# AdaLN and an eight-expert MoE on one core: the copy of x into the output as one transfer, started earlier, and one VectorE step moved ahead of another

## The chip, the cores and the metric

The kernel runs on one core of a Trainium2 chip. Its time is the device time of one execution in microseconds (us). The kernel before was timed three times: 1524.31, 1526.02 and 1527.0 us, with a median of 1526.02 us. The engines are called by the names of the profile: PE (TensorE, the matrix engine; PEld is its weight load), DVE (VectorE), ACT (ScalarE), POOL (GpSimd) and SP (SyncE, which here only issues transfers). All transfers, whoever issues them, run on the core's 16 DMA engines.

## The reference, cut to what matters

```
styles = w @ (affine_w * gain).T + affine_b            # 8 x 512
y      = einsum('blc,oc->blo', x * styles, weight) * rsqrt(sum((weight*styles)**2)) 
y      = clip(y + bias, -256, 256)                     # 4096 tokens of 512
scores = softmax(y @ Wr)                               # 8 experts
G, idx = top_k(scores.T, 1024)                         # each expert takes 1024 tokens
h      = gelu(einsum('ekd,edh->ekh', y[idx], W1) + b1) # 512 -> 2048
X_e    = einsum('ekh,ehd->ekd', h, W2) + b2            # 2048 -> 512
out    = x + zeros.at[idx].add(G * X_e)                # x is the kernel's input
```

The last line is what the change touches: the output holds a copy of the input x, 4096 rows of 512 float32 (8.39 MB), to which each expert's rows are added.

## The kernel before, in words

Every matmul is done on float32 values split into a high and a low part ("hi", "lo"), three matmuls for one product. The parts are made by ACT (hi, a copy) and DVE (lo, a subtraction), and PE waits for both by semaphores. The five engines each run a list of instructions that is written out by hand, so the order in the code is the order on the engine, and a waiting instruction holds up all that stand behind it on its engine.

Stages, with their times in the profiled execution: the style matmuls and the router (to about 130 us), the choice of expert 0's tokens (to about 166 us), expert 0 in 32 blocks of work (to about 345 us), then seven more experts, each with a hidden part (8 steps of seven products, a Strassen-like scheme in which DVE adds products in PSUM) and an output part (16 chunks).

Expert 0. Block i has a matmul group `A(i)` (12 matmuls, line 1548) and a group `B(i-2)` (12 matmuls, line 1593); between them PE takes a small step of the threshold search for the other experts (`count`, lines 1485 and 1487), which needs DVE's counts (line 1031). ACT makes, in this order, the hi part of W1 for block i+2 (`w1_hi`, line 666), the hi part of W2 (`w2_hi`, line 674) and the two gelus (lines 806, 807). DVE makes, in this order, `w1_lo` (line 1129), `w2_lo` (line 1134), the lo part of the hidden values (line 1289) and then the counts of the search. The weights come by 256 KB loads that SP issues (`load_w1`, line 369; `load_w2`, line 374), three buffers each; among them SP issues transposes of gathered rows (`transposes`, line 437).

POOL gathers expert 0's rows in eight indirect transfers (line 529), and then copies x into the output in four pieces of 1024 rows (line 560). The first piece waits for the second round of SP's transposes (`s_xt`), and piece q for `A(7 + 2q)` of PE (`s_A`). All later writes to the output (the scatters, line 544) wait for all four pieces (`s_o0`).

Experts 1 to 7. In step g the DVE does `u2`, `c12` of the step before, `u3` (line 1217: product 7 plus product 1 into U3) and `c22_c21` (line 1222: adds U3 to two banks). PE's product `P3(g)` adds into one of these banks and waits for `c22_c21(g)` (semaphore `s_cc`). At the end of the hidden part (k = 7) PE runs P1, P6, P3 of the step before, P7, P5, P4, P2, then the first tile of the first output chunk (`chunk(16 * n, (0,))`, line 1664), then `P3(8 * n + 7)`, then the rest of the chunk. DVE makes the lo parts for that first chunk in `chunk_lo` (lines 1234 and 1238), once ACT has made the hi parts (`chunk_hi`, lines 767 and 771).

Of the kernel before, what the change touches and what calls it, by code (L numbers as in the profile page):

```python
# [5 lines left out]
def adaln_moe_kernel(nc, xT, x, condT, WT, biasT, affWT, affbT, WrT, W1, b1T, W2, b2, out):  # L6
# [26 lines left out]
    with ctx:  # L33
# [3 lines left out]
        def sem(name):  # L37
            return ctx.enter_context(nc.semaphore(name))
# [172 lines left out]
        def asf(ap):  # L211
            return ap.bitcast(f32)
# [9 lines left out]
        def w2slot(j):  # L222
            return RG[:, j % 2, 0:1024].rearrange("p (l n) -> p l n", l=2)

        def hslot(j):
            return RG[:, j % 2, 1024:3072].rearrange("p (l n) -> p l n", l=2)
# [51 lines left out]
        s_xt = [sem(f"s_xt{i}") for i in range(4)]  # L278
# [7 lines left out]
        s_o0 = sem("s_o0")  # L286
# [26 lines left out]
        s_A = sem("s_A")  # L313
# [32 lines left out]
        s_gat = [sem(f"s_gat{i}") for i in range(4)]  # L346
# [127 lines left out]
        def _(eng):  # L474
# [79 lines left out]
                gather(c, 0, c)  # L554

            for i in range(4):
                eng.wait_ge(s_xt[i], 32)
            for q in range(4):
                eng.wait_ge(s_A, 8 + 2 * q)
                eng.dma_start(out[1024 * q:1024 * q + 1024, :], x[1024 * q:1024 * q + 1024, :]).then_inc(s_o0, 16)  # L560
            eng.wait_ge(s_o0, 64)
            for t in range(4):
                scatter(t, 0, t, OB[:, t, :])
            gather_pairs(0)
# [292 lines left out]
        def _(eng):  # L857
# [247 lines left out]
            def build_oh(e, q):  # L1105
                if e:
                    eng.wait_ge(s_im, 4 * e)
                if e == 2 and q == 0:
                    eng.wait_ge(s_sc, 128)
                eng.tensor_tensor((OH0 if e < 2 else OHx)[:, q, :, :],  # L1110
                                  (slo[:, 8 * q:8 * q + 8, e:e + 1] if e else
                                   slo0[:, 8 * q:8 * q + 8, None]).broadcast_to([128, 8, 128]),
                                  io128[:, None, :].broadcast_to([128, 8, 128]), ALU.is_equal).then_inc(s_oh, 1)

            def finish_idx(e):
                eng.wait_ge(s_im, 4 * e + 4)
                v = list_bank(e)[:, 0:40].rearrange("p (v h) -> p h v", v=5)
                with nc.allow_low_precision(reason="token numbers below 4096 are exact"):
                    eng.tensor_reduce(idx[:, e, :], v[:, :, 0:2], AX.X, ALU.add).then_inc(s_idx, 1)
                eng.tensor_reduce(G[:, e, :], v[:, :, 2:5], AX.X, ALU.add).then_inc(s_imc, 1)  # L1120
# [16 lines left out]
            def x_lower(r):  # L1137
                eng.wait_ge(s_xt[r % 4], 16 * (r // 4 + 1))
                if r < 10:
                    if r >= 2:  # L1140
                        eng.wait_ge(s_xh, r - 1)
                        eng.wait_ge(s_xl, r - 1)
                else:
                    eng.wait_ge(s_xhr, (r - 8) // 2)
                    eng.wait_ge(s_xlr, (r - 8) // 2)
                if r >= 16 and (r - 8) % 8 == 0:
                    eng.wait_ge(s_hlo, 2 * (r - 8) - 16 + 6)
                eng.tensor_copy(halves(r)[:, :, 0], XU[:, r % 4, 4:8, :].rearrange("p c n -> p (c n)")).then_inc(s_il, 1)
# [29 lines left out]
            def sums(g):  # L1178

                u = g + 8 * (g // 8)  # L1180
                r = RAW[:, u % 3, :, :]
                eng.wait_ge(s_raw[u % 3], 32 * (u // 3 + 1))
                if g:
                    eng.wait_ge(s_wls, g)
                else:
                    eng.wait_ge(s_A, NBLK)
                chain[0] += 1
                first = chain[0]
                eng.tensor_tensor(ST[:, 0, :], r[:, 0, :], r[:, 1, :], ALU.add).then_inc(s_v, 1)
                eng.tensor_tensor(ST[:, 2, :], r[:, 0, :], r[:, 2, :], ALU.subtract)  # L1190
                eng.wait_ge(s_v, first)
                link(eng.tensor_tensor(ST[:, 1, :], ST[:, 0, :], r[:, 2, :], ALU.subtract))
                eng.tensor_tensor(ST[:, 3, :], r[:, 3, :], ST[:, 1, :], ALU.subtract).then_inc(s_sS, 1)

            def lo_raw(g):
                u = g + 8 * (g // 8)
                eng.wait_ge(s_whr, g + 1)
                eng.tensor_tensor(wslot(g)[:, 1, 0:3, :], RAW[:, u % 3, 1:4, :], asf(wslot(g)[:, 0, 0:3, :]),  # L1198
                                  ALU.subtract).then_inc(s_wlr, 1)

            def lo_S(g):
                eng.wait_ge(s_whs, g + 1)
                eng.wait_ge(s_sS, g + 1)
                eng.tensor_tensor(wslot(g)[:, 1, 3:7, :], ST[:, :, :], asf(wslot(g)[:, 0, 3:7, :]),  # L1204
                                  ALU.subtract).then_inc(s_wls, 1)

            def banks(g):
                return (Pt, BBt)[g % 2]

            def u2(g):  # L1210
                eng.wait_ge(s_cp1, g + 1)
                eng.wait_ge(s_P[6], g + 1)
                eng.tensor_tensor(U2(g), banks(g)[:, PB, :], P1C, ALU.add).then_inc(s_u2, 1)

            def u3(g):
                eng.wait_ge(s_P[7], g + 1)
                eng.tensor_tensor(U3, banks(g)[:, PB, :], P1C, ALU.add).then_inc(s_u3, 1)

            def c22_c21(g):
                eng.wait_ge(s_P[4], g + 1)  # L1220
                eng.wait_ge(s_u3, g + 1)
                eng.tensor_tensor(banks(g)[:, PB:PD + 1, :], banks(g)[:, PC:PD + 1:2, :],
                                  U3[:, None, :].broadcast_to([128, 2, 512]), ALU.add).then_inc(s_cc, 1)

            def c12(g):
                eng.wait_ge(s_P[3], g + 1)
                eng.wait_ge(s_u2, g + 1)
                eng.tensor_tensor(banks(g)[:, PC, :], banks(g)[:, PC, :], U2(g), ALU.add).then_inc(s_c12, 1)

            def chunk_lo(jj):  # L1230
                n, j = jj // 16, jj % 16
                u = 16 * n + 8 + j // 2
                eng.wait_ge(s_v2h, jj + 1)
                eng.tensor_tensor(w2slot(j)[:, 1, :], RAW[:, u % 3, :, :].rearrange("p b n -> p (b n)")  # L1234
                                  [:, 512 * (j % 2):512 * (j % 2) + 512], asf(w2slot(j)[:, 0, :]),
                                  ALU.subtract).then_inc(s_v2l, 1)
                eng.wait_ge(s_hh, jj + 1)
                eng.tensor_tensor(hslot(j)[:, 1, :], H[:, j, :], asf(hslot(j)[:, 0, :]),  # L1238
                                  ALU.subtract).then_inc(s_hlo, 1)
# [84 lines left out]
            for n in range(NX):  # L1324
                for k in range(8):
                    g = 8 * n + k
                    if 0 < k < 7:
                        lo_raw(g + 1)
                    u2(g)
                    if k:  # L1330
                        c12(g - 1)
                    else:
                        sums(g + 1)
                        lo_raw(g + 1)
                    if k == 5 and n + 2 < E:
                        finish_idx(n + 2)
                    u3(g)
                    if k == 7:
                        chunk_lo(16 * n)
                    if k < 7:  # L1340
                        lo_S(g + 1)
                    if n + 2 < E and 1 <= k <= 4:
                        build_oh(n + 2, k - 1)
                    c22_c21(g)
                    if k < 6:
                        sums(g + 2)
                c12(8 * n + 7)
                for j in range(1, 16):
                    chunk_lo(16 * n + j)
                    if n + 3 < E and j == 3:  # L1350
                        build_rhs(n + 3)
                    if n + 1 < NX and j in (6, 8, 10, 12):
                        x_lower(16 + 8 * n + j - 6)
                        x_lower(17 + 8 * n + j - 6)
                        xp_sums(4 * n + 4 + (j - 6) // 2)
                    if n + 1 < NX and j in (7, 9, 11, 13):
                        xp_lo(4 * n + 4 + (j - 7) // 2)
                    if j == 14 and n + 1 < NX:
                        sums(8 * n + 8)
                if n + 1 < NX:  # L1360
                    lo_raw(8 * n + 8)
                for t in range(4):
                    evac(n, t)
                if n + 1 < NX:
                    lo_S(8 * n + 8)
                for t in range(4, 8):
                    evac(n, t)
# [389 lines left out]
```

## Time and profile before

| | before |
|---|---|
| median of 3 runs | 1526.02 us |
| the profiled execution's own time | 1526.02 us |
| its span | 1523.8 us |
| outside the span | 2.2 us |
| PE busy | 1467.0 us, 96% |
| DVE busy | 1005.5 us, 66% |
| ACT busy | 729.8 us, 48% |
| POOL busy | 190.4 us, 12% |
| mean granted PE clock | 0.982 |
| bytes moved | 164.40 MB, mean 108 GB/s |

How to read it: the span runs from the first to the last instruction of the profiled execution. "Busy" is the time in which an engine executes; "idle before" is what it waited for. The clock is the share of full speed that was granted to PE. A transfer's "landing" is the time from its issue to its completion semaphore. A busy share near 1 in a stretch says that the stretch is bound by that engine.

### The profile page before, as it was taken

The numbers are of one execution on the slowest core, as the hardware profiler recorded it, in microseconds if no ns is written. First come the engines' busy times: TensorE is split into PE (matmuls) and PEld (weight loads), VectorE is DVE, ScalarE is ACT, GpSimd is POOL, SyncE is SP. The second block draws the span as 40 slices with busy tenths as digits, with TensorE's granted clock in tenths as the row PEclk, the third lists the DMA queues.
The fourth block names the chain that finished last, engine by engine and source line by source line (L and its number), as shares of the span: only waits on it lengthen the run. The fifth ranks groups of instructions, "written<-read, shape, count | busy, mean of one in ns | idle before, by whom it ended". The sixth has DMA issues, their size and how long they took to land.

```text
span 1523.8 us, 18932 instructions
## 1 busy us (share of the span) xinstructions
PE 1467.0 (96%) x6759; PEld 1199.9 (79%) x6759; DVE 1005.5 (66%) x1687; ACT 729.8 (48%) x986; POOL 190.4 (12%) x161
## 2 busy tenths in 40 slices
PE   8994699999999999999999999999999999999995
PEld 6773577888888888888888888888888888888884
DVE  5666677678746785668657774678567864776432
ACT  5773444365435544454445443554445444544322
POOL 0000300211011301102020301130110202030003
PEclk9997799999999999999999999999999999999998
DMA  6874656494116431525143511543152515251104
GB/s 218 240 194 111 166 179 229 124 187 118 56 55 139 92 85 51 145 65 118 42 131 77 132 56 59 135 101 87 49 146 61 112 42 141 67 125 56 42 28 56
DMA packets 166252, 164.40 MB, mean 108 GB/s; under 512 B 109584, under 2 KB 109712, under 8 KB 165136
## 3 DMA queue, kind: packets, MB, share of 16 engines
q1 hardware_dynamic: 151632, 121.24, 28.8%
q0 software_dynamic: 14528, 41.95, 12.7%
q8 instruction: 55, 0.90, 0.2%
q14 instruction: 37, 0.30, 0.1%
HBM read 112.82 MB, written 33.55 MB: 96 GB/s over the span
## 4 chain that ended last, share of the span: by engine, by line
PE 95%; DVE 2%; DMA 1%; POOL 1%; issue 1%; ACT 0%; POOLq 0%; SPq 0%; DVEq 0%; ACTq 0%
PE BBt L1664 20%; PE Pt L1664 20%; PE BBt L1604 18%; PE Pt L1604 17%; PE BBt L1593 5%; PE Pt L1548 5%; PE BBt L1401 5%; PE Pt L1432 1%; PE BBt L1413 1%; PE Pt L1444 1%; DMA XB<-in_xT 0%; POOL out L544 0%; DVE XF L989 0%; DVE OH L1110 0%; PE BBt L1577 0%
## 5 line engine op out<-in xcount | busy, mean ns | idle before, releaser
L1664 PE MATMUL Pt<-RG 128*128 128x512 f32 x1344 | 324.2, 389 | 0.0
L1664 PE MATMUL BBt<-RG 128*128 128x512 f32 x1344 | 323.5, 390 | 0.0
L1664 PEld LDWEIGHTS BBt<-RG 128*128 128x128 f32 x1344 | 251.7, 188 | 54.7 <-issue 2.7
L1664 PEld LDWEIGHTS Pt<-RG 128*128 128x128 f32 x1344 | 251.9, 188 | 53.0 <-issue 0.5
L1604 PE MATMUL BBt<-XT,RG 128*128 128x512 f32 x1176 | 281.1, 390 | 0.0
L1604 PE MATMUL Pt<-XT,RG 128*128 128x512 f32 x1176 | 279.1, 389 | 0.0
L1604 PEld LDWEIGHTS Pt<-XT,RG 128*128 128x128 f32 x1176 | 220.7, 188 | 45.8
L1604 PEld LDWEIGHTS BBt<-XT,RG 128*128 128x128 f32 x1176 | 220.0, 188 | 46.0
L1234 DVE TENSOR_TENSOR RG<-RAW,RG 128x512 fp32r<-128x512 f32 x112 | 77.6, 693 | 195.5 <-ACT RG L767 194.8
L767 ACT ACTIVATE RG<-RAW 128x512 fp32r<-128x512 f32 x112 | 70.7, 631 | 272.1 <-PE BBt L1664 269.6
L1238 DVE TENSOR_TENSOR RG<-H,RG 128x1024 fp32r<-128x1024 f32 x112 | 137.3, 1226 | 28.7 <-ACT RG L771 27.2
L544 POOL DMA_INDIRECT out<-OBx,idx x56 | 89.1, 1591 | 463.6 <-DVE OBx L1245 448.6
L529 POOL DMA_INDIRECT XR<-y_rows,idx x64 | 74.5, 1165 | 573.6 <-issue 440.9
L725 ACT ACTIVATE RG<-RAW 128x768 fp32r<-128x768 f32 x56 | 47.4, 847 | 169.4 <-PE BBt L1604 76.3
L771 ACT ACTIVATE RG<-H 128x1024 fp32r<-128x1024 f32 x112 | 117.0, 1045 | 0.0
L731 ACT ACTIVATE RG<-ST 128x1024 fp32r<-128x1024 f32 x56 | 59.3, 1060 | 96.3 <-PE Pt L1604 36.9
L1593 PE MATMUL BBt<-W2S,HS 128*128 128x512 f32 x360 | 88.3, 394 | 0.0
L1401 PE MATMUL BBt<-XC,WHL 128*128 128x512 f32 x336 | 79.7, 392 | 0.7 <-ACT YT L591 0.7
L1593 PEld LDWEIGHTS BBt<-W2S,HS 128*128 128x128 f32 x360 | 66.5, 188 | 13.2
L1401 PEld LDWEIGHTS BBt<-XC,WHL 128*128 128x128 f32 x336 | 62.4, 188 | 14.6 <-ACT YT L591 1.1
L1204 DVE TENSOR_TENSOR RG<-ST,RG 128x1024 fp32r<-128x1024 f32 x56 | 68.1, 1217 | 0.3 <-ACT RG L731 0.3
L1198 DVE TENSOR_TENSOR RG<-RAW,RG 128x768 fp32r<-128x768 f32 x56 | 53.3, 952 | 21.2 <-ACT RG L725 21.2
(223 smaller groups left out, 1556.4 us busy)
## 6 DMA issues: line engine op xcount, KB each, us to landing
RAW<-in_W SPq DMA_DIRECT2D x224, 256.0 KB
W1R<-in_W SPq DMA_DIRECT2D x32, 256.0 KB, 3.8
W2R<-in_W SPq DMA_DIRECT2D x32, 256.0 KB, 3.3
y_rows<-XR SPq DMA_DIRECT2D x32, 256.0 KB, 2.6
XB<-in_xT SPq DMA_DIRECT2D x7, 1024.0 KB, 5.2
B<-in_b SPq DMA_DIRECT2D x8, 256.0 KB, 7.5
WTraw<-in_WT SPq DMA_DIRECT2D x4, 256.0 KB, 6.9
XB<-in_xT SPq DMA_DIRECT2D x4, 256.0 KB, 7.5
```

The source lines that it names most:

```text
L529: eng.indirect_dma_start(XR[:, r % 4, :], None, y_d[:, :], bass.IndirectOffsetOnAxis(idx[:, e, c:c + 1], 0), bounds_check=NT * 128 - 1, oo ...
L544: eng.indirect_dma_start(out[:, :], bass.IndirectOffsetOnAxis(idx[:, e, c:c + 1], 0), src, None, bounds_check=NT * 128 - 1, oob_is_err=Tru ...
L767: eng.activation(w2slot(j)[:, 0, :], RAW[:, u % 3, :, :].rearrange("p b n -> p (b n)") [:, 512 * (j % 2):512 * (j % 2) + 512], ACT.Copy).t ...
L771: eng.activation(hslot(j)[:, 0, :], H[:, j, :], ACT.Copy).then_inc(s_hh, 1)
L1204: eng.tensor_tensor(wslot(g)[:, 1, 3:7, :], ST[:, :, :], asf(wslot(g)[:, 0, 3:7, :]), ALU.subtract).then_inc(s_wls, 1)
L1234: eng.tensor_tensor(w2slot(j)[:, 1, :], RAW[:, u % 3, :, :].rearrange("p b n -> p (b n)") [:, 512 * (j % 2):512 * (j % 2) + 512], asf(w2sl ...
L1238: eng.tensor_tensor(hslot(j)[:, 1, :], H[:, j, :], asf(hslot(j)[:, 0, :]), ALU.subtract).then_inc(s_hlo, 1)
L1401: last = mm(BB[o][:, :], wt(a, c)[:, 128 * o:128 * o + 128], XC[:, b % 2, d, c, :], start=(c == 0 and n == 0), stop=(c == 3 and n == 2))
L1548: last = mm(AB[i % 2][:, :], W1S[:, i % 3, a, 128 * c:128 * c + 128], XT0[u][:, d, c, :], start=(c == 0 and n == 0), stop=(c == 3 and n == 2))
L1593: last = mm(BB[t][:, :], HS[:, i % 3, a, 128 * t:128 * t + 128], W2S[:, i % 3, d, :], start=(j == 0 and n == 0), stop=(j == NJ - 1 and n = ...
L1604: last = mm((Pt, BBt)[g % 2][:, bank, :], wslot(g)[:, a, w, 128 * k:128 * k + 128], XT[:, b, d, k, :], start=(begins and k == 0 and m == 0 ...
L1664: last = mm((Pt, BBt)[t // 4][:, t % 4, :], hslot(j)[:, a, hcol(t):hcol(t) + 128], w2slot(j)[:, d, :], start=(j == 0 and m == 0), stop=(j ...
```

## The change

Two places are changed. POOL's copy of x into the output becomes one transfer of 8.39 MB in place of four of 2.1 MB. It waits for the second round of gathers (`s_gat`) in place of the second round of transposes and of PE's blocks 8 to 14. And on DVE, in the last hidden step (k = 7) of each of the experts 1 to 7, `chunk_lo(16 * n)` stands ahead of `u3(g)` in place of behind it.

```
             for i in range(4):
-                eng.wait_ge(s_xt[i], 32)
-            for q in range(4):
-                eng.wait_ge(s_A, 8 + 2 * q)
-                eng.dma_start(out[1024 * q:1024 * q + 1024, :], x[1024 * q:1024 * q + 1024, :]).then_inc(s_o0, 16)
-            eng.wait_ge(s_o0, 64)
+                eng.wait_ge(s_gat[i], 32)
+            eng.dma_start(out.rearrange("(a b) d -> a (b d)", a=512),
+                          x.rearrange("(a b) d -> a (b d)", a=512)).then_inc(s_o0, 16)
+            eng.wait_ge(s_o0, 16)
             for t in range(4):
                 scatter(t, 0, t, OB[:, t, :])
...
                     if k == 5 and n + 2 < E:
                         finish_idx(n + 2)
-                    u3(g)
                     if k == 7:
                         chunk_lo(16 * n)
+                    u3(g)
                     if k < 7:
                         lo_S(g + 1)
```

POOL's instructions around the copy, before (XR are the gathered rows, OB the first rows to scatter; the two numbers are the access pattern, 32 runs of 16384 float32, 64 KB each):

```order
L529 DMA XR<-y_rows,idx 128x1024 x8
L560 DMA out<-in_x 32x16384 x4
L544 DMA out<-OB,idx 4096x512 x4
L529 DMA XR<-y_rows,idx 128x1024 x8
```

And in the changed kernel, whose lines 556 to 560 are one line fewer:

```order
L529 DMA XR<-y_rows,idx 128x1024 x8
L558 DMA out<-in_x 128x16384
L544 DMA out<-OB,idx 4096x512 x4
L529 DMA XR<-y_rows,idx 128x1024 x8
```

The runs of the copy stay 64 KB long, 128 of them in one transfer where there were 32 in each of four.

DVE's instructions at the end of expert 1's hidden part, before (PU holds U2 and U3, RG the split operands, BBt and Pt the PSUM banks):

```order
L1213 TENSOR_TENSOR PU<-BBt,PU 128x512
L1228 TENSOR_TENSOR Pt<-Pt,PU 128x512
L1217 TENSOR_TENSOR PU<-BBt,PU 128x512
L1234 TENSOR_TENSOR RG<-RAW,RG 128x512
L1238 TENSOR_TENSOR RG<-H,RG 128x1024
L1222 TENSOR_TENSOR BBt<-BBt,PU 128x1024
```

And in the changed kernel (every line number behind the copy is one less):

```order
L1212 TENSOR_TENSOR PU<-BBt,PU 128x512
L1227 TENSOR_TENSOR Pt<-Pt,PU 128x512
L1233 TENSOR_TENSOR RG<-RAW,RG 128x512
L1237 TENSOR_TENSOR RG<-H,RG 128x1024
L1216 TENSOR_TENSOR PU<-BBt,PU 128x512
L1221 TENSOR_TENSOR BBt<-BBt,PU 128x1024
```

`u3` moves from ahead of the two subtractions of `chunk_lo` to behind them, directly ahead of `c22_c21`, which reads its result. PE, ACT and SP have the same order of instructions as before.

## Rows read from the trace of the kernel before

**Rows 1.** The page: span of the profiled execution.
```profile
span 1523.8 us, 18932 instructions
```

**Rows 2.** Busy time by stretch: engines, granted clock, DMA share, GB/s.
```profile
181.00:260.00 79.00, 79.00 (x367) 62.03 (x367) 55.75 (x209) 39.82 (x68) 2.11 (x4) 1.00 0.68 222
345.00:1500.00 1155.00, 1155.00 (x5255) 953.08 (x5254) 769.02 (x1060) 539.03 (x667) 140.43 (x100) 1.00 0.34 86
```

**Rows 3.** Timeline at expert 1's last hidden step: start, length, engine, operation.
```profile
428.66 0.69 DVE L1217 TENSOR_TENSOR PU<-BBt,PU 128x512 f32<-128x512 f32 x1 [0.66 <-PE BBt L1604]
429.70 0.69 DVE L1234 TENSOR_TENSOR RG<-RAW,RG 128x512 fp32r<-128x512 f32 x1 [0.35 <-ACT RG L767]
430.65 1.22 DVE L1238 TENSOR_TENSOR RG<-H,RG 128x1024 fp32r<-128x1024 f32 x1 [0.26 <-ACT RG L771]
431.79 1.23 DVE L1222 TENSOR_TENSOR BBt<-BBt,PU 128x1024 f32<-128x1024 f32 x1
...
432.54 0.84 PE L1664 MATMUL Pt<-RG 128*128 128x512 f32 x3
433.22 1.52 PE L1604 MATMUL BBt<-XT,RG 128*128 128x512 f32 x6
```

**Rows 4.** The same place in the last expert.
```profile
1417.56 1.23 DVE L1222 TENSOR_TENSOR BBt<-BBt,PU 128x1024 f32<-128x1024 f32 x1
...
1418.99 1.30 PE L1604 MATMUL BBt<-XT,RG 128*128 128x512 f32 x5
```

**Rows 5.** Timeline of POOL: the last gather, and the copy's second piece.
```profile
176.89 1.18 POOL L529 DMA_INDIRECT XR<-y_rows,idx  x1 [1.54 <-DMA XU<-XR]
224.36 0.54 POOL L560 DMA_DIRECT2D out<-in_x  x1 [10.64 <-PE Pt L1548]
```

**Rows 6.** Landing of that gather, then of the four pieces.
```profile
DMA to landing us min/median/max: 3.6/3.6/3.6
...
DMA to landing us min/median/max: 8.7/9.6/10.4
```

**Rows 7.** DMA queues, 213 to 216 us, 216 to 219 us: packets, MB, share.
```profile
q0 software_dynamic: 16, 1.05, 98.6%
...
q0 software_dynamic: 16, 1.05, 91.4%
```

**Rows 8.** DMA queues between 226 and 231.5 us (second piece).
```profile
q1 hardware_dynamic: 3, 0.00, 0.1%
```

**Rows 9.** SP's issues during the second piece; landing of the W1R load.
```profile
229.23 0.33 SPq L369 DMA_DIRECT2D W1R<-in_W  x1
229.83 4.07 SPq L374 DMA_DIRECT2D W2R<-in_W  x1
...
DMA to landing us min/median/max: 5.5/5.5/5.5
```

**Rows 10.** W2R load issued at 247.0 us: its landing.
```profile
DMA to landing us min/median/max: 8.6/8.6/8.6
```

**Rows 11.** SP's issue (a transpose) while the last gather lands.
```profile
179.99 1.90 SPq L437 DMA_TRANSPOSE XU<-XR  x1
```

**Rows 12.** Expert 0's block 4: ACT, then DVE, then PE.
```profile
190.38 0.63 ACT L666 ACTIVATE W1S<-W1R 128x512 fp32r<-128x512 f32 x1
195.62 0.68 ACT L807 ACTIVATE HS<-Pt,b 128x512 fp32r<-128x512 f32 x1
...
196.33 0.69 DVE L1289 TENSOR_TENSOR HS<-HF,HS 128x512 fp32r<-128x512 f32 x1 [2.01 <-ACT HS L807]
198.56 0.09 DVE L1031 DVE_READ_ACCUMULATOR OB<-OB,cand 128x1 bf16 x1
...
200.87 0.18 PE L1487 MATMUL Pt<-cnt,BOS 128*128 128x3 bf16 x1
```

**Rows 13.** Busy time by stretch (columns as in rows 2) where the clock falls.
```profile
130.00:131.00 1.00, 0.93 (x6) 0.96 (x7) 0.00 (x0) 0.96 (x2) 0.00 (x0) 0.69 0.00 0
```

**Rows 14.** PE at 167 us: fourteen matmuls, most at the lower clock.
```profile
166.97 5.50 PE L1678 MATMUL Pt<-YH,IR 128*128 128x512 f32 x14
```

## The prediction, made before the changed kernel ran

> **What bounds the kernel now.** I read the busy times by stretch first. From 181 to 260 us PE is busy for 79.00 of 79 us, and from 345 to 1500 us for 1155.00 of 1155, all at the full clock [rows 2]. So from 181 us on the time is PE's: nothing that becomes faster elsewhere can bring the end forward, and whatever makes PE wait moves the end by as much. The profiled execution's own time is 1526.02 us, its span 1523.8 us [rows 1], 2.2 us lie outside; it is also the median of the runs, so the sum below is made against 1526.0. For each of the two edits the question is then which PE instruction waits for something that gets later. I read the timeline at both places, and for the copy the DMA queues in short windows.
>
> **Edit 2, the DVE order at k = 7, seven times.** Before: `u3` runs from 428.66 to 429.35, DVE then waits for ACT until 429.70, makes the two subtractions of `chunk_lo` (the second ends at 431.87) and `c22_c21` from 431.79 to 433.02 [rows 3]. PE starts `P3(7)` at 433.22, 0.20 us after that. It stands right behind the three matmuls of the chunk's first tile, which began at 432.54 and at about 0.23 us each would be through at 433.22: PE just makes it, with no slack that I can see [rows 3]. The last expert has the same picture, 1417.56 + 1.23 = 1418.79 and P3 at 1418.99 [rows 4]; all seven places agree within 0.03 us.
> After: `chunk_lo` can't start earlier than 429.70, because it was ACT that it waited for and not `u3`. The 0.35 us of idle time that `u3` now leaves empty in front of it is lost. `u3` starts at 431.79, where `c22_c21` started, and `c22_c21` one `u3` later. Instructions follow each other 0.08 us before the end of the last (431.79 against 431.87), so a `u3` of 0.69 costs 0.61 us. P3 starts 0.61 us later and PE has nothing else to do: it is in order, and the rest of the chunk stands behind P3. What hangs on P3 (ACT's gelus, the banks of the chunk's other tiles) moves with it. What could be won is `chunk_lo`'s result, needed by the first tile at 432.54; it is ready at 431.87 in both orders. Cost 7 x 0.61 = 4.3 us. Bounds: 0, if P3 has a slack that the modelled matmul ends hide; 7 x 0.69 = 4.8. I take 4.3, since the dependency is direct.
>
> **Edit 1, what the copy did.** Its four pieces ran between 213 and 257 us, in which PE never waited [rows 2]. Taking them away from there wins nothing. A piece is 32 runs of 64 KB. In the DMA queues the first piece shows as 16 packets with 1.05 MB in 213 to 216 us and 16 more in 216 to 219 us: one packet of 64 KB on each of the 16 engines, twice. Their share of 3 us is 98.6% and 91.4%, so 2.96 and 2.74 us for one packet, mean 2.85 [rows 7]. A piece lands 8.7 to 10.4 us after its issue [rows 6]; less two packets (5.7) that is 3.0 to 4.7 us of start and completion.
> While a piece is in progress the loads of SP's queue stand still. Between 226 and 231.5 us, queue q1 has 3 packets, where one 256 KB load alone has 128 [rows 8]. The W1R load issued at 229.23 lands 5.5 us later, at 234.7; the piece was issued at 224.36 and landed at most 10.4 us later, at 234.8. The W2R behind it can't even be issued: SP spends 4.07 us in it [rows 5, 6, 9]. A load issued at 247.0, 0.6 us ahead of the fourth piece, took 8.6 us [rows 10]: what a piece overtakes waits for both of its packets, not for one. Before this was harmless, as a piece is over in two packets and the weight buffers are three deep.
> The Trainium skill ("DMA: Bandwidth & Descriptors", section "Queues, rings and completion order") says that an engine takes the queues in turn, but drains a whole packet, typically 9 to 17 descriptors, before it switches. These rows agree as far as they go: two descriptors passed in one turn. By that rule the 8 of the new transfer could too.
>
> **Edit 1, when the copy runs now.** The last gather is issued at 176.89 and lands 3.6 us later, at 180.5 [rows 5, 6]; nothing else holds POOL. One transfer of 128 packets is 8 on each engine, 8 x 2.85 = 22.8 us, so it lands 22.8 + (3.0 to 4.7) = 25.8 to 27.5 us after its issue at 180.6: 206.4 to 208.1, middle 207.3. At that moment SP is in the transpose that it issues from 179.99 to 181.89 [rows 11]. The W1 load of block 6 stands behind that on SP, and on the DMA queue behind both. The new transfer's packets reach the engines about 1.5 us after its issue, near 182. I take that the transpose is caught in the middle, and the load wholly.
>
> **Edit 1, who waits.** ACT takes `w1_hi(6)` at 190.38 [rows 12], and behind it, in order, stand the gelus of block 4, behind these DVE's lo part (196.33), then its counts, the last at 198.56, and for these PE waits ahead of `B(3)` with its search matmul at 200.87 [rows 12]. PE still has work up to there (A(4), B(2), A(5)), and then stops. The path from the landing of the W1 load to that matmul: `w1_hi` and `w2_hi` 1.35 us (0.63 each, and W2's load is issued a little later), two gelus 1.3 (0.68 each, overlapping a little), from the start of DVE's lo part to its last count 198.65 - 196.33 = 2.3, PE's start 0.15; together 5.1 us. The load lands at 207.3 plus what is left of the transpose's issue (up to 1.9) and a load behind it: between 207 (as the W1R load of rows 9 did, together with the piece) and 212. I take 210. PE resumes at 210 + 5.1 = 215.1; stall 215.1 - 200.9 = 14.2 us, bounds 11 to 16. Should one of the 16 engines also hold back the W1 load of block 5, which SP issues just ahead of that transpose, PE would stop one block earlier, at 200.9 - 5.8 = 195.1 (a block is 27 matmuls, and 367 of them take 79 us [rows 2]), and resume at 207.3 + 5.1 = 212.4: 17 us.
> Then the clock. It falls from 1.00 towards 0.50 (2.4 to 1.2 GHz) in the slice 130 to 131 us, at the router's end, where PE has only small matmuls with gaps between them [rows 13]. When it has to come back, at 166.97 us, fourteen full matmuls take 5.50 us [rows 14]; at the full clock's 0.23 us they would take 3.2. That is 2.3 us lost until PE is at full speed. A stall of 14 us without any matmul should do the same. Bounds 0 and 3; I take 2.2.
> Nothing behind it waits twice: the next loads land 2 to 3 us apart, and a block takes PE 5.8 us. The other waits of the edit cost nothing: the scatters that wait for the whole copy come after block 17.
>
> Sum: 1526.0 + 4.3 + 14.2 + 2.2 = 1546.7, about 1547 us. Of its own this case spans 1541 to 1553.
>
> **The rivals.**
> A. The queues take turns: between two 64 KB packets, SP's queue gets one of its loads through. Then the transposes and loads from 182 to 206 us come at one per 3 us or so, about 8 in 23 us, where 10 are wanted. The load of block 6 would have to land by 200.9 - 5.1 = 195.8, 13.8 us after its issue; it would. No stall, only edit 2: 1526.0 + 4.3 = 1530.3. For it: the landing at 247.0 + 8.6 concerns a few packets only. Against it: three packets of q1 in 5.5 us. The skill's rule of turns, in the same section, taken by single packets rather than by 9 to 17 descriptors, would give this.
> B. What SP has issued by 183 us gets ahead of the copy (block 6's load too), and only block 7's is caught. It is wanted 5.8 us later, by 201.6, and lands at about 211: a stall of 9.5, and 1526.0 + 4.3 + 9.5 + 2.2 = 1542.
> C. The copy is slower in one piece than in four. At a piece's whole 9.6 us it takes 38 us and lands at 219; the stall is 12 us longer: 1559.
> D. On the other side, not slower: the place is P3 behind `c22_c21`. If the semaphore reaches PE with 0.6 us or more to spare, which the profile's modelled matmul times would not show, edit 2 is free; with A's turns as well, the kernel stays at 1526. It decides at a slack of 0.6 us. The 0.20 us that P3 starts after `c22_c21`'s end at all seven places, back to back with the matmul before, allow a little slack and speak against 0.6.
>
> **How the numbers follow.** The forecast has 0.66, A 0.14, B 0.10, C 0.06, D 0.04. A measurement of this kernel can tell 0.2%, 3 us, from no change. All but D lie above 1529; A at 1530.3 is close to that bound, so same gets 0.05, faster 0.01, slower 0.94. The range reaches from 1530 (with most of A) over B to 1555, and leaves out C, D and the edge of A.
>
> **What would show it.** In the changed kernel's profile: one POOL transfer out<-in_x at about 181 us with a landing of 26 to 28 us; 128 packets of 64 KB; an SP issue of more than 15 us near 180 to 183 us; hardly a q1 packet between 184 and 204 us; a PE wait of 11 to 17 us at the search matmul (or at a block 4 to 6 matmul), PE's clock at 0.5 around 200 to 220 us; the last expert's P3 starting 0.6 us later behind the chunk's first tile, in all seven experts. Wrong is the first part if q1 goes on moving loads through the copy, and the second if P3 still follows the first tile without a gap.

## The result and the profile after

| | before | after |
|---|---|---|
| median | 1525.37 us (4 runs, 1524.31 to 1527.0) | 1580.77 us (4 runs, 1568.92 to 1583.64) |
| ratio, 95% interval | 1 | 1.0348 (1.0294 to 1.0401) |
| the profiled execution's own time | 1526.02 us | 1582.52 us |
| its span | 1523.8 us | 1580.6 us |
| mean granted PE clock | 0.982 | 0.967 |

The kernel became slower, as forecast, but by 55 us where 21 were forecast, and the time lies outside the range of 1530 to 1555. Repeated in two more jobs (below) the same kernel took 1547 us (median) and 1557 us: its time is drawn anew in each execution. The ratios leave out executions that were classed as slow (1582.5, 1575.0, 1592.6 and 1597.5 us), which here are high draws of the kernel itself, and therefore all single times are given below.

PE, the granted clock, POOL's transfer and SP's issues around it, in the timeline after (start, length, engine, operation):

```profile
198.89 0.20 PE L1484 MATMUL Pt<-KC,KR 1*128 1x3 bf16 x2
250.07 0.19 PE L1486 MATMUL Pt<-cnt,BOS 128*128 128x3 bf16 x1 [50.98 <-DVE OB L1030]
250.28 5.38 PE L1592 MATMUL BBt<-W2S,HS 128*128 128x512 f32 x12
...
179.23 0.61 POOL L558 DMA_DIRECT2D out<-in_x  x1 [3.02 <-DMA XR<-y_rows,idx]
...
180.95 0.57 SPq L369 DMA_DIRECT2D W1R<-in_W  x1
182.17 58.72 SPq L437 DMA_TRANSPOSE XU<-XR  x1
...
245.22 0.63 ACT L665 ACTIVATE W1S<-W1R 128x512 fp32r<-128x512 f32 x1 [56.59 <-DMA W1R<-in_W]
245.88 0.69 DVE L1128 TENSOR_TENSOR W1S<-W1R,W1S 128x512 fp32r<-128x512 f32 x1 [54.61 <-ACT W1S L665]
```

PE stops at the very matmul of [rows 12] (there line 1487, now 1486), for 50.98 us. The chain behind it is the forecast one: ACT sits idle 56.59 us for the W1 load of block 6, DVE for ACT, PE for DVE's counts. The path from ACT's start, 245.22, to PE's, 250.07, takes 4.85 us. The twelve matmuls behind the wait take 5.38 us where they took 2.99: the lower clock, 2.4 us. What is new is SP: a transpose (of the second round) whose issue takes 58.72 us, and the copy itself. The W1 load issued at 180.95 lands 64.2 us later; the landing of POOL's transfer is

```profile
DMA to landing us min/median/max: 65.8/65.8/65.8
```

where 25.8 to 27.5 us were forecast. The DMA queues in 185 to 200 us after (q0 is POOL's, q1 is SP's: packets, MB, share of 16 engines), and the busy times by stretch (PE, PEld, DVE, ACT, POOL, clock, DMA share, GB/s):

```profile
q0 software_dynamic: 18, 1.18, 144.0%
q1 hardware_dynamic: 67, 0.02, 89.9%
...
200.00:223.00 23.00, 0.00 (x0) 0.00 (x0) 0.00 (x0) 0.00 (x0) 0.00 (x0) 0.59 0.25 30
```

In [rows 7] 16 packets passed in each 3 us; now 18 start in 15 us, and from 200 to 223 us the core moves 30 GB/s, though most of the copy still waits. From 223 to 240 us it is 370 GB/s. The packets' own records say what happened: from 185 to 202 us one engine starts a 64 KB packet every 2.43 us, with exactly one 256-byte packet of the transpose between two of them; on the other engines the transpose's packets take 2.43 or 4.85 us each and end together, 0.3 us behind the end of each of the first engine's 64 KB packets. Their own first packets of the copy last from where they began until 222 or 223 us, up to 37 us; only one of them ends earlier, at 203.4. From there to 220.4 a second engine does the same with its packets. Only then do the others move on, together. So, as these times read, the engines that carry a transpose advance in step, and one that has 64 KB packets in turn with it sets the step for all.

The second edit, at expert 1's last hidden step, after:

```profile
483.58 0.69 DVE L1216 TENSOR_TENSOR PU<-BBt,PU 128x512 f32<-128x512 f32 x1
484.37 1.23 DVE L1221 TENSOR_TENSOR BBt<-BBt,PU 128x1024 f32<-128x1024 f32 x1
...
484.33 0.84 PE L1663 MATMUL Pt<-RG 128*128 128x512 f32 x3
485.66 1.66 PE L1603 MATMUL BBt<-XT,RG 128*128 128x512 f32 x6 [0.49 <-DVE BBt L1221]
```

P3 starts 1.33 us behind the first tile's matmul, where it was 0.68 [rows 3]: 0.65 us later, and its second matmul follows the first after 0.34 us where it was 0.23, so that the group ends another 0.11 later. The last expert shows the same 1.33 (1474.64 to 1475.97). From the first matmul of expert 1 to the last of the kernel it is 1149.94 us before and 1155.34 after: 5.4 us, 0.77 for each place.

Sum of the profiled executions: 50.98 + 2.4 + 5.4 = 58.8; in this execution PE came to the search matmul 1.85 us earlier (198.89 for 200.74), so 56.9. Measured: 1582.52 - 1526.02 = 56.5.

### The profile page after: what moved, and what is told of

Its sections match the earlier page's. It is cut to its first block, busy times and chain, and to the rows that moved or that the text cites. A ratio compares the mean times of both kernels' runs of the same rounds, so it can differ in the third digit from the quotient of the medians.

```text
span 1580.6 us, 18929 instructions
## 1 busy us (share of the span) xinstructions
PE 1471.5 (93%) x6759; PEld 1201.8 (76%) x6759; DVE 1005.1 (64%) x1687; ACT 730.0 (46%) x986; POOL 189.2 (12%) x158
## 4 chain that ended last, share of the span: by engine, by line
PE 89%; another core or an unknown queue 4%; DVE 4%; issue 1%; ACT 1%; DMA 1%; POOL 1%; POOLq 0%; SPq 0%; DVEq 0%; ACTq 0%
PE BBt L1663 19%; PE Pt L1663 19%; PE Pt L1603 17%; PE BBt L1603 15%; PE BBt L1592 5%; PE BBt L1400 5%; PE Pt L1547 5%; PE Pt L1431 1%; PE BBt L1412 1%; DVE BBt L1221 1%; DVE RG L1237 1%; PE Pt L1443 1%; ACT RG L770 0%; POOL out L544 0%
## 5 line engine op out<-in xcount | busy, mean ns | idle before, releaser
L544 POOL DMA_INDIRECT out<-OBx,idx x56 | 89.2, 1592 | 463.6 <-DVE OBx L1244 448.7
```

What stands on the lines that cost most here:

```text
L544: eng.indirect_dma_start(out[:, :], bass.IndirectOffsetOnAxis(idx[:, e, c:c + 1], 0), src, None, bounds_check=NT * 128 - 1, oob_is_err=Tru ...
```

## The experiments

All lines of the table are medians with the single times, in us; the first median is without the profiled execution (1582.5). The kernel before took 1524.1 to 1525.4 (medians) beside them.

| kernel | median | single times | ratio, 95% |
|---|---|---|---|
| changed kernel, 1st | 1580.8 | 1568.9, 1580.0, 1581.5, 1582.5, 1583.6 | 1.0348 (1.0294 to 1.0401) |
| e1_copy_only | 1550.7 | 1542.0, 1542.4, 1559.1, 1575.0 | 1.0168 (1.0116 to 1.0220) |
| e2_order_only | 1530.1 | 1529.6, 1530.1, 1530.1, 1530.9, 1533.6 | 1.0034 (1.0021 to 1.0048) |
| e3_one_late | 1536.2 | 1534.7, 1535.8, 1536.6, 1536.9 | 1.0071 (1.0055 to 1.0086) |
| e4_early_2kb | 1534.9 | 1534.6, 1534.6, 1535.2, 1536.0 | 1.0067 (1.0051 to 1.0082) |
| e5_after_again | 1547.0 | 1545.7, 1546.9, 1547.1, 1549.6 | 1.0140 (1.0125 to 1.0155) |
| e6_copy_only_again | 1543.0 | 1541.1, 1542.5, 1542.8, 1543.2, 1552.1, 1592.6 | 1.0131 (1.0109 to 1.0153) |
| e7_early_transposes_later | 1541.4 | 1540.1, 1541.1, 1541.6, 1542.0 | 1.0105 (1.0091 to 1.0120) |
| e8_late_2kb | 1524.0 | ten, 1523.3 to 1525.8 | 0.9994 (0.9985 to 1.0003) |
| e9_first_piece_early | 1533.8 | 1523.9, 1531.8, 1535.9, 1536.7 | 1.0064 (1.0049 to 1.0079) |
| e10_u3_between | 1525.8 | eleven, 1525.4 to 1528.9 | 1.0007 (0.9998 to 1.0016) |
| e11_after_third | 1556.6 | 1546.9, 1547.6, 1549.6, 1563.6, 1566.5, 1597.5 | 1.0180 (1.0145 to 1.0214) |
| e12_transposes_later_again | 1539.9 | 1539.2, 1539.8, 1539.9, 1543.5 | 1.0107 (1.0093 to 1.0122) |

### e1_copy_only and e2_order_only: which edit

Each has one edit of the change and nothing else.

> The copy's edit alone, with the DVE order of before. The theory after the first trace (coupling): in the changed kernel the copy landed 65.8 us after its issue, because SP's transposes were on the same DMA engines; a transpose gave up one 256-byte packet for each 64 KB packet of the copy on one engine, and the other engines moved on only in step with it. By it this kernel has nearly all of the loss: 1525.4 + about 50 (44 to 55), a landing over 50 us, PE's wait about 51 us. The rival (two edits that make each other worse): clearly less than the changed kernel's 1580.8 less 5.4, so under 1565. The model of the prediction (24 to 28 us landing): 1542.

> The DVE order's edit alone, with the copy of before. The changed kernel's trace shows P3 at 0.65 us later in each of seven places, and its second matmul another 0.11 later, so 0.76 x 7 = 5.3 to 5.4 us: 1530.8, ratio 1.0035. By the prediction's term it is 4.3 (ratio 1.0028). If the cost belonged to the disturbed run and not to the order, it would be nothing.

e2 is 1.0034: 5.3 us as the trace said, and its span from expert 1's first matmul is the changed kernel's, 1155.34. e1 was a surprise: not 1575 each time, but 1542, 1542, 1559, 1575. The profile fell on one of the 1542 us. In it the copy, POOL's transfer, landed in

```profile
DMA to landing us min/median/max: 29.6/29.6/29.6
...
215.11 0.19 PE L1486 MATMUL Pt<-cnt,BOS 128*128 128x3 bf16 x1 [14.75 <-DVE OB L1030]
```

and PE's wait was 14.75 us at the same matmul, with 5.36 us for the twelve behind it, so nearly what the prediction had worked out (14.2 and 2.2). The queues in 185 to 200 us in this execution:

```profile
q0 software_dynamic: 80, 5.24, 103.4%
q1 hardware_dynamic: 79, 0.16, 3.3%
```

80 packets of the copy in 15 us: all engines in parallel. And 79 packets of SP's queue: one for one. An engine with both queues waiting takes one packet of each in turn, whatever their size, so SP's queue gets 2 KB or less for each 64 KB. That is a starved queue, not a blocked one.

### e3_one_late: the same transfer with no transpose in flight

```
             for i in range(4):
-                eng.wait_ge(s_gat[i], 32)
+                eng.wait_ge(s_xt[i], 32)
```
(against e1)

> One transfer of 8.39 MB in 64 KB runs as in the changed kernel, but issued when the second round of transposes has landed (about 193 us), so that no transpose is in flight with it; DVE order of before. Coupling theory: the landing is 26 to 30 us, as 8 packets of 2.4 to 2.9 us on each engine in parallel; SP's weight loads still get one 2 KB packet for each 64 KB packet, so the load that SP issues at about 194 lands near 221 where PE needs it by about 213: a PE wait of 6 to 12 us, with the clock 1532 to 1540. Rival (a transfer of this size from HBM to HBM is slow in itself): a landing of about 60 us and 1565 or more. Rival (weight loads get through between packets): a landing of 26 to 30 us and no PE wait, 1525.

The copy is issued at 193.25 and lands 28.5 us later; PE waits 8.48 us three blocks later than in e1, and the four times lie within 2.2 us. The queues between 196 and 218 us: 110 packets and 110 packets. The weight loads issued meanwhile take 21.5 us. Size, then, is not the reason for 65.8 us, and a transfer in one piece starves SP's queue also when it runs late.

```profile
q0 software_dynamic: 110, 7.21, 98.3%
q1 hardware_dynamic: 110, 0.23, 3.1%
...
W1R<-in_W SPq DMA_DIRECT2D x2, 256.0 KB, 21.5
```

### e4_early_2kb and e8_late_2kb: the copy in runs of 2 KB

```
-            eng.dma_start(out.rearrange("(a b) d -> a (b d)", a=512),
-                          x.rearrange("(a b) d -> a (b d)", a=512)).then_inc(s_o0, 16)
+            eng.dma_start(out.rearrange("(a b) d -> b a d", b=128),
+                          x.rearrange("(a b) d -> b a d", b=128)).then_inc(s_o0, 16)
```
(e4 against e1, waits for `s_gat`; e8 against e3, waits for `s_xt`)

> The copy as one transfer as early as in the changed kernel (behind the gathers), but in 4096 runs of 2 KB instead of 128 of 64 KB; DVE order of before. If engines take SP's and POOL's queues in turns of one packet each, a turn now costs 0.1 us instead of 2.4: transposes and weight loads land within about 10 us of their issue, no PE wait or a small one, 1525 to 1530, the copy's landing 30 to 50 us. Rival (it is the bytes in flight or HBM that are short, or POOL's queue has priority): PE waits as in the changed kernel, over 1550.

> One transfer in 2 KB runs, issued once the transposes have landed (about 193 us). With 64 KB runs this cost 10.7 us. Theory of turns by the packet: SP's weight loads now get a 2 KB packet for each 2 KB packet of the copy, so they land within 6 us, PE doesn't wait: 1524 to 1526, landing of the copy 28 to 36 us. Rival (bytes in flight): a PE wait of 6 to 10 us, 1533 or more.

e8's time came out as expected: no wait of PE behind the copy, 0.9994. Its copy lands in 35.0 us, slower than e3's 28.5, and its weight loads in 7.7 us (W1) and 9.4 (W2), slower than the 6 expected, where e3's took 21.5. e4 was a miss by half: the four times lie within 1.5 us, but PE still waits 8.77 us. Between 190 and 205 us e4's queues have 1118 packets of the copy and 1117 of SP's, nearly all of 256 bytes. The copy's packets are of 4 KB here, not of 2 KB as both expectations took it (4.58 MB in 1118 packets), and take 0.16 us each: a turn holds two of the runs. A transpose has 1024 packets, 64 for each engine, and with a 4 KB packet ahead of each it lasts (SP was 18.04 us in the issue of one). Taking turns by the packet hurts the one with the small packets, even at 4 KB to 256 bytes.

```profile
q0 software_dynamic: 1118, 4.58, 91.0%
q1 hardware_dynamic: 1117, 0.39, 10.7%
```

e8's W1 loads between 196 and 218 us:

```profile
W1R<-in_W SPq DMA_DIRECT2D x4, 256.0 KB, 7.7
```

### e5_after_again, e6_copy_only_again, e11_after_third: chance or program

The changed kernel and e1 once more without any edit.

> The changed kernel once more, on one chip with the next three. Its first five times were 1568.9 to 1583.6, those of the copy's edit alone 1542 to 1575, though the two kernels run the same instructions in the same order up to 345 us. Theory (chance): how many DMA engines take the copy one after the other, while the others stand still behind a transpose's packet, changes from execution to execution; each such engine costs 8 packets of 2.4 us, about 19 us. Then this kernel's times spread like those of the copy's edit alone plus 5.4: some of them near 1548. Rival (the code's placement or the DVE edit decides it): all again near 1570 to 1584.

> The copy's edit alone once more, beside the changed kernel. Chance: 1542 to 1580 again, overlapping with the changed kernel less 5.4. Rival: its times lie below all of the changed kernel's by far more than 5.4.

> The changed kernel a third time, beside the next. By the theory of chance its times have a lower cluster near 1547 (no engine takes the copy alone) and higher ones up to about 1595; by the nine times so far about half are over 1560. If all of a job's times stand together again, the chance is drawn for the chip or the job and not for each execution.

Chance. Over the three jobs (a job is one set of runs on one chip: the first result, e5, e11) the changed kernel took 1545.7 to 1549.6 us in 7 of 15 executions and 1563.6 to 1597.5 in 8; the copy's edit alone 1541.1 to 1543.2 in 6 of 10 and 1552.1 to 1592.6 in 4. The lower clusters differ by about 5 us, the second edit. Job 1 had the changed kernel's high times only, job 2 its low ones only, job 3 both; so the draw may lean with the chip or the job, but it isn't fixed by it. The profiles of e11 and e5 show the steps between: POOL's transfer lands in 31.4 us in e5's (1549.6 us), and in e11's (1566.5 us) in

```profile
DMA to landing us min/median/max: 45.2/45.2/45.2
```

There one engine took its eight packets alone from 185.6 to 205.5, and the other fifteen stood still in their first packets of the copy, from 185.8 to 206.8. From 29.6 us (e1) over 45.2 to 65.8, where two engines did so, each adds 16 to 21 us, near the 8 x 2.43 = 19.4 us of an engine's eight packets. The times of 1552 and of 1592 to 1598 us have no profile; that they are the same thing is inferred.

The packets' records also tell the high profiles from the low ones. The transpose in flight when the copy is issued has 1024 packets of 256 bytes. In the four low profiles with it (e1, e5, e6 and e9's, there for the first piece) the copy's first packet starts 3.0 to 3.7 us after its issue, and the transpose's last packet starts within 0.2 us of it: hardly anything of the transpose is left to be held up. In e11's the copy's first packet starts 2.4 us after the issue, and 12 packets of the transpose are left when all engines have begun with the copy; eight of them come one by one behind the packets of the engine that ran alone. In the first profile it starts after 1.6 us, when 479 of the 1024 have started. What differs between these six profiles is thus how far the transpose has come when the copy reaches the engines.

### e7_early_transposes_later and e12_transposes_later_again: no transposes beside the early copy

```
-                if i < 7:
-                    transposes(i + 1)
+                if 7 <= i < 11:
+                    transposes(i - 3)
```
(SP's list, against e1)

> The copy's edit alone, and SP's four transposes of the second round moved from blocks 3 to 6 to blocks 7 to 10, so that none is in flight with the copy. Coupling theory: the copy lands in 25 to 29 us, PE waits 10 to 16 us for block 6's W1 load, and the spread is gone: 1536 to 1542 in all runs, within 3 us. Rival (a copy issued this early is slow or variable by itself): times over 1550 among them.

> The early copy without transposes in flight again, more runs: by the coupling theory every time within 3 us of 1541, none over 1546, while the kernels with transposes in flight went over 1550 in 9 of 19 executions. One time over 1550 here would speak for a copy that is variable by itself.

Eight executions, 1539.2 to 1543.5, none high, where 12 of 25 were high with transposes in flight; in the same two jobs it was 5 of 16, so the times alone leave a little room for chance. The lower cluster's cost stays: PE waits 14.7 us (e7's profile). In 185 to 200 us the queues have 71 packets each, and a W1 load issued in that time takes 25.1 us.

### e9_first_piece_early: a quarter of the copy, early

```
             for i in range(4):
-                eng.wait_ge(s_xt[i], 32)
+                eng.wait_ge(s_gat[i], 32)
             for q in range(4):
-                eng.wait_ge(s_A, 8 + 2 * q)
+                if q:
+                    eng.wait_ge(s_A, 8 + 2 * q)
```
(against the kernel before)

> The kernel before, but the first of the four pieces is issued behind the gathers as in the changed kernel, beside the transposes; the other three wait for PE's blocks 10, 12 and 14 as before. Two packets of 64 KB for each engine. Coupling theory: a transpose is held up by 5 us for one engine's two packets, more if engines go one after the other, but the weight loads have 13.8 us to spare: mostly no PE wait, 1524 to 1526, now and then up to 1535. Rival (the early place costs by itself, whatever the size): 1540.

One execution at 1523.9, three at 1531.8 to 1536.7. The profile is of the first: no wait, and 5.98 us for the transpose's issue. So two packets for each engine are enough for a loss when a transpose is in flight, and more often than expected. The loss of 7 to 12 us is more than expected, too, since the forecast had 13.8 us of slack for a delay of 5. No profile of a high one was taken; that its loss is the same standing in step is inferred.

### e10_u3_between: half of the second edit

```
                 eng.tensor_tensor(w2slot(j)[:, 1, :], ..., ALU.subtract).then_inc(s_v2l, 1)
+                if between is not None:
+                    u3(between)
                 eng.wait_ge(s_hh, jj + 1)
```
(in `chunk_lo`, at k = 7 only, against the kernel before)

> The kernel before, with u3 at k = 7 between the two subtractions of chunk_lo: it fills DVE's wait of 0.26 us for ACT instead of the one of 0.35. c22_c21 should end 0.61 - 0.35 = 0.26 us later than before, and P3's restart costs as in the changed kernel another 0.04 + 0.11: 0.42 x 7 = 2.9 us, ratio 1.0019 (the full edit: 1.0034). If the cost came from the reordering as such and not from c22_c21's lateness: 5.4 us here too, or none.

1.0007, and 1151.44 us from expert 1's first matmul to the kernel's last: 1.5 us more than before, half of the 2.9 expected. At expert 1:

```profile
433.35 1.23 DVE L1222 TENSOR_TENSOR BBt<-BBt,PU 128x1024 f32<-128x1024 f32 x1
...
433.85 0.89 PE L1667 MATMUL Pt<-RG 128*128 128x512 f32 x3
434.63 1.65 PE L1607 MATMUL BBt<-XT,RG 128*128 128x512 f32 x6
```

Measured from the first tile's start, `c22_c21` ends at 0.73 us (it was 0.48 in [rows 3]), so 0.25 later as expected. But P3 starts only 0.10 us later, 0.05 us behind `c22_c21`'s end, where it was 0.20 before. The kernel before had 0.15 us of slack at this place.

## Why the prediction was right or wrong

**What bounds the kernel: right.** PE; both losses are waits of PE, and nothing was won where the pieces had been.

**Edit 2, 4.3 us: the mechanism right, the term too small.** It cost 5.3 to 5.4 us (e2, and both spans). Three parts were mis-sized. `u3` delays `c22_c21` not by 0.61 but by 0.79 us (483.58 to 484.37), since `c22_c21` reads U3 and waits for its end, where two independent operations overlap by 0.08. The slack of P3 was 0.15 us and not nothing. And a matmul group that has waited ends 0.11 us later than its wait. 0.79 - 0.15 + 0.11 = 0.75, seven times 5.3. e10 agrees: 0.25 - 0.15 + 0.11 = 0.21, seven times 1.5.

**Edit 1, who waits and through which chain: right.** The matmul at which PE stops, the W1 load of block 6, the chain over ACT and DVE (4.85 us, forecast 5.1), the clock (2.4 us, forecast 2.2): all came close to the forecast.

**Edit 1, how long the copy lasts: the step that failed.** "One transfer of 128 packets is 8 on each engine, 8 x 2.85 = 22.8 us, so it lands [...] 25.8 to 27.5 us after its issue." This takes the sixteen engines as independent of each other. They were in [rows 7], where no transpose was in flight. The copy now starts while SP's transposes of the second round are: that was written down ("the transpose is caught in the middle"), but costed only as a load queued later. In the traces a caught transpose makes its engines advance in step, and an engine that serves the copy alone holds up the other fifteen for its eight packets, about 19 us. With none such the landing is 29.5 to 31.4 us and the changed kernel takes 1546 to 1550 us, near the forecast; with one 45.2 us and 1566; with two 65.8 us and 1582. e7 and e12 take the transposes away and the spread with them. None of the rivals was this; C had a slow copy at 1559, for another reason, and was given 0.06.

**Turns.** The forecast and rival A disagreed on whether SP's queue gets turns during a long copy. It does, from the first packet on, one for one (80 and 79, 110 and 110, 71 and 71 packets). But a turn is one packet, 2 KB or 256 bytes, and 8 turns are one weight load's. So the starvation was right and its picture (a queue that stands still) was not. That block 6's load landed at 210.4 us in e1, where 210 was forecast, is partly luck: it needs eight turns on each engine, and the copy has eight packets there. The rows that spoke for the picture did not bear on it: SP issued no load between 223.8 and 229.2 us, so for most of the window of [rows 8] its 3 packets are those of an empty queue, not of one that stood still. The trace of before even has the turns, though not in a row that was read: at the fourth piece three 2 KB packets of SP's queue start at 251.71, 251.91 and 252.21 us, each where a first packet of the copy ends, and each ends where a second one starts (251.79, 251.99, 252.29). The prediction's reading that two descriptors passed in one turn does not hold there. The Trainium skill ("DMA: Bandwidth & Descriptors", section "Queues, rings and completion order") has the turns at packet granularity, with 9 to 17 descriptors in a typical packet. The turns agree; here each turn was a single packet of 64 KB (4 KB in e4) against a single one of 2 KB or 256 bytes.

**The range.** It held all of the lower cluster, and I had given 0.66 to one outcome as though it would come out the same each time. That executions of one kernel could differ by 50 us was not considered; the kernel before varies by 5 at most within a job. As a loss the lower cluster is 22.1 us (e5, against 1524.85 beside it) where the forecast was 20.7. Of the 1.4 us between them about 1 is the second edit; the forecast's base, 1526.0, lies 1.2 above the kernel before in that job, so that the totals agree better than the terms.

What stays open: why the copy's first packets start 1.6 to 3.7 us after its issue from execution to execution, how the transpose couples the engines, and why the first job drew high in all five. The packets' records don't name their engine; that one engine after the other takes the copy is read from the start and end times of its packets.

## What to carry to other kernels

Before moving a transfer, look at which other transfers will be in flight with it, and how long the longest single packet is, not only how many bytes. Queues take turns by the packet: large runs next to a queue with small ones (weight loads, and above all transposes) starve the small ones, and cutting the large ones into runs of 2 KB made the same copy harmless where no transpose was in flight (e8), not where one was (e4, 8.77 us of waiting). A wait of an in-order engine that "just makes it" is worth an experiment with half the delay: e10 gave the slack, 0.15 us, that the timeline alone did not.

## What the hardware showed that was not expected

- A DMA transpose kept its 16 engines in step: with another queue's 64 KB packets beside it, its 256-byte packets took 2.43 or 4.85 us on the other engines, multiples of one engine's copy packet (2.42 us), and the core moved 30 GB/s for 23 us.
- SP was held for 58.7 us in the issue of one transpose, and every load behind it in its list with it.
- The same program, on one chip, took between 1546.9 and 1597.5 us; its one profile there (1566.5 us) shows this standing in step.
- HBM to HBM, 8.39 MB in one transfer: landing 28.5 us in 64 KB runs, 35.0 us in 2 KB runs with the weight loads passing beside it.
